# Graph attention: features and turned probabilities in fp32, one fp32 product per block in place of three fp16 products

## The reference, cut to what matters

```
h   = relu(layernorm(x))
Wh  = h @ W                                # the features
src, dst = Wh @ a[:F], Wh @ a[F:]          # two scores a node
att = softmax(where(adj > 0, leaky_relu(src + dst.T), -9e15), axis=1)
h_prime = att @ Wh                         # the product that is changed
gi, gh = h_prime @ w_ih.T + b_ih, h @ w_hh.T + b_hh
r, z, n = ...                              # gates and candidate of the GRU
x = x + (1 - z) * n + z * h
```

## Time and profile before

| | |
|---|---|
| median of 3 runs | 3374.41 us (3373.42 to 3374.91) |
| time of the profiled execution | 3378.01 us |
| its span, first to last instruction | 3376.3 us |
| `attention_features`, first product to last score column | about 51 to 95 us in the span |
| `gat_gru`, first adjacency tile to last update | about 120 to 609 us |
| PE, DVE, ACT busy over the whole span | 74%, 63%, 38% |

### The profile page before, as it was taken

The page is one execution under the profiler, slowest core; times in us unless marked ns, Lnnn a source line. Parts: engine busy times, 40 slices in busy tenths (PEclk is TensorE's granted clock), DMA queues, the critical chain, the costliest instruction groups (busy, mean ns, idle before and its releaser), DMA issues. The chain is left out here.

```text
span 3376.3 us, 47607 instructions
## 1 busy us (share of the span) xinstructions
PE 2512.2 (74%) x14938; PEld 1795.0 (53%) x14938; DVE 2112.2 (63%) x5159; ACT 1270.4 (38%) x2109; POOL 588.6 (17%) x1525
## 2 busy tenths in 40 slices
PE   3488888395749997968754596397748159999999
PEld 2366667384527775757623375275537024444458
DVE  5578887413246667673237777777785767777751
ACT  4455554303256564632245375275532320000000
POOL 0000000000033333320025364264430000000000
PEclk9699999697759998989856797697879579999999
DMA  1222220021000000000100000000000130000013
GB/s 41 105 87 90 92 96 30 25 63 47 15 1 16 20 23 14 17 20 16 39 15 5 5 14 14 5 14 9 9 9 10 37 101 0 0 0 0 0 33 96
DMA packets 44330, 104.10 MB, mean 31 GB/s; under 512 B 5584, under 2 KB 24304, under 8 KB 41328
## 3 DMA queue, kind: packets, MB, share of 16 engines
q1 hardware_dynamic: 44144, 102.05, 9.3%
HBM read 85.46 MB, written 16.58 MB: 30 GB/s over the span
## 5 line engine op out<-in xcount | busy, mean ns | idle before, releaser
L1206 PE MATMUL bank<-kT,step_queries 64*128 64x512 f32 x528 | 285.4, 693 | 315.1 <-ACT step_E L1273 299.8
L1705 DVE SCALAR_TENSOR_TENSOR fil_acc<-bank,fil_node,fil_acc 128x256 f32<-128x256 f32 x682 | 329.9, 484 | 109.9 <-PE bank L1778 97.3
L1206 PEld LDWEIGHTS bank<-kT,step_queries 64*128 64x128 f32 x528 | 107.5, 228 | 491.0 <-ACT step_E L1273 413.2
L1273 ACT ACTIVATE step_E<-bank 128x512 f32<-128x512 f32 (+1 forms) x264 | 137.4, 545 | 412.6 <-PE bank L1206 209.8
L1776 PE MATMUL bank<-fil_wh,fil_xTh 128*128 128x512 f16 x704 | 268.1, 381 | 0.0
L1777 PE MATMUL bank<-fil_wl,fil_xTh 128*128 128x512 f16 x704 | 267.9, 380 | 0.0
L1778 PE MATMUL bank<-fil_wh,fil_xTl 128*128 128x512 f16 x704 | 267.8, 380 | 0.0
L1293 ACT ACTIVATE step_junk<-step_E,step_first 128x2708 fp8e4<-128x2708 f32 x88 | 224.6, 2552 | 14.7 <-ACT step_bell L1300 8.9
L1386 DVE MAX8 step_top<-step_E 128x8 f32<-128x2708 f32 x44 | 131.2, 2982 | 132.9 <-ACT step_E L1273 128.4
L1223 PE MATMUL bank<-H,step_PT 128*128 128x256 f32 x968 | 212.6, 379 | 0.8 <-ACT step_PT L1264 0.8
L1223 PE MATMUL bank<-A,step_PT 128*128 128x256 f32 x968 | 212.6, 379 | 0.7 <-ACT step_PT L1264 0.7
(11 more groups left out here) (339 smaller groups left out, 5433.6 us busy)
## 6 DMA issues: line engine op xcount, KB each, us to landing
gat_A<-in_adj SPq DMA_DIRECT2D x22, 1408.0 KB, 6.1
step_a<-adjT SPq DMA_DIRECT2D x44, 352.0 KB, 3.1
fil_raw<-in_L_W SPq DMA_DIRECT2D x16, 512.0 KB, 4.8
adjT<-gat_a SPq DMA_DIRECT2D x22, 352.0 KB, 2.2
gcn_a<-adjT SPq DMA_DIRECT2D x22, 352.0 KB, 3.0
out_a<-adjT SPq DMA_DIRECT2D x22, 352.0 KB, 2.9
X<-in_x SPq DMA_DIRECT2D x1, 2816.0 KB, 10.9
x_kept<-X SPq DMA_DIRECT2D x1, 2816.0 KB, 9.8
```

The lines of the kernel that those rows point to most:

```text
L1206: pe.matmul(l_bank[n % 2][:, 0:m], queries[q][half, :], kT[half, c:c + m], start=True, stop=True).then_inc(l_ready, 1)
L1273: act.activation(E[q][j][:, c:c + m], l_bank[n % 2][:, 0:m], ACT.Copy).then_inc(l_done, 1)
L1705: c(dve.scalar_tensor_tensor(out=acc[k][:], in0=ps, scalar=node[k][:, n:n + 1], in1=acc[k][:], op0=ALU.mult, op1=ALU.add))
```

## The change

The features are kept as fp32 rows `V` (ACT copies the bank, no low half on DVE). The turned probabilities are copied by ACT as fp32 into `PT`, which takes the same memory as the four fp16 halves did; DVE's six low halves a tile go. The product of a block is one fp32 matmul call. The waits on `lo_done` become waits on `pT_done`, which ACT's copy raises. The scale factors of the fp16 parts go. `probabilities_times`, which nothing called, is deleted.

```diff
-            def high(t, k):
+            def rows(t, k):
                 act.wait_ge(wh_ready, t + 1)
-                core.fence(act)
-                act.activation(hi(HLw, t), wh_bank[k][:, 0:D], ACT.Copy, scale=SH).then_inc(hi_done, 1)
+                act.activation(cols(V, t), wh_bank[k][:, 0:D], ACT.Copy).then_inc(rows_done, 1)
...
                 reuse(dve, scored, t, 2)
-                dve.wait_ge(hi_done, t + 1)
-                dve.scalar_tensor_tensor(out=lo(HLw, t), in0=ps, scalar=SH, in1=hi(HLw, t),
-                                         op0=ALU.mult, op1=ALU.subtract)
+                dve.wait_ge(rows_done, t + 1)
...
-        PhT = [core.HL[:, k * NP:(k + 1) * NP] for k in range(2)]
-        PlT = [core.HL[:, (2 + k) * NP:(3 + k) * NP] for k in range(2)]
+        PT = [core.HL[:].bitcast(F32)[:, k * NP:(k + 1) * NP] for k in range(2)]
...
-            lows = [(1, lambda t, k, n=n: low(t, k, n)) for n in range(NCH)]
-            pipelined(dve, [(3, take_product), (0, mask), *lows[0:2], (1, row_scale), (6, update), (4, gates),
-                            (5, candidate), lows[2], (0, larger), *lows[3:5], (0, probabilities), lows[5]])
+            pipelined(dve, [(3, take_product), (0, mask), (1, row_scale), (6, update), (4, gates),
+                            (5, candidate), (0, larger), (0, probabilities)])
...
-                act.activation(PhT[k][:, b * 128:(b + m) * 128], p_bank[n % 2][:, 0:m * 128],
-                               ACT.Copy, scale=SP).then_inc(hi_done, 1)
+                act.activation(PT[k][:, b * 128:(b + m) * 128], p_bank[n % 2][:, 0:m * 128],
+                               ACT.Copy).then_inc(pT_done, 1)
...
-                    pe.wait_ge(lo_done, t * NCH + n - 1)
+                    pe.wait_ge(pT_done, t * NCH + n - 1)
...
                 if n == 0:
-                    pe.wait_ge(lo_done, t * NCH + NCH)
+                    pe.wait_ge(pT_done, t * NCH + NCH)
...
-                    pe.matmul(ps, PhT[k][:, blk], hi(HLw, j), start=j == 0, stop=False)
-                    pe.matmul(ps, PhT[k][:, blk], lo(HLw, j), start=False, stop=False)
-                    last = pe.matmul(ps, PlT[k][:, blk], hi(HLw, j), start=False, stop=j == T - 1)
+                    last = pe.matmul(ps, PT[k][:, blk], V[:, j * D:j * D + D], start=j == 0, stop=j == T - 1)
```

More of the change, by code:

```diff
@@ L39 @@
 SH = 1024.0
-SP = 8192.0
 SX = 8.0
@@ L316, in times_weight, with attention_features @@
     return last
-def attention_features(core, HLw, S, dB, dpB, dmin, W, a):
+def attention_features(core, V, S, dB, dpB, dmin, W, a):
     nc, HL, idh = core.nc, core.HL, core.idh
@@ L325, in attention_features @@
         sem = lambda n: nc.alloc_semaphore(f"wh_{n}")
-        loaded, xt_ready, xT_ready, wh_ready, hi_done, scores, scored, rep_ready, dB_done, tail, stored = (
-            sem(n) for n in ("loaded", "xt_ready", "xT_ready", "wh_ready", "hi_done", "scores", "scored",
+        loaded, xt_ready, xT_ready, wh_ready, rows_done, scores, scored, rep_ready, dB_done, tail, stored = (
+            sem(n) for n in ("loaded", "xt_ready", "xT_ready", "wh_ready", "rows_done", "scores", "scored",
                              "rep_ready", "dB_done", "tail", "dB_ready"))
@@ L371, in evacuate @@
                 act.activation(xT[k][:], xt_bank[k][:, 0:D], ACT.Copy, scale=1 / SH).then_inc(xT_ready, 1)
-            def high(t, k):
+            def rows(t, k):
                 act.wait_ge(wh_ready, t + 1)
-                core.fence(act)
-                act.activation(hi(HLw, t), wh_bank[k][:, 0:D], ACT.Copy, scale=SH).then_inc(hi_done, 1)
-            pipelined(act, [(0, evacuate), (1, high)])
+                act.activation(cols(V, t), wh_bank[k][:, 0:D], ACT.Copy).then_inc(rows_done, 1)
+            pipelined(act, [(0, evacuate), (1, rows)])
             for n, (b, m) in enumerate(CHUNKS):
@@ L410, in _ @@
             dve.tensor_scalar(dpB[:], dB[:], dmin[:, 0:1], None, ALU.subtract)
[L413 to L421, removed]
 def adjacency_times(pe, ps, a8, V, start=True):
@@ L431, in adjacency_times, with gat_gru @@
     return last
-def gat_gru(core, HLw, S, dpB, dmin, adj, adjT8, w_ih, w_hh, b_ih, b_hh):
+def gat_gru(core, V, S, dpB, dmin, adj, adjT8, w_ih, w_hh, b_ih, b_hh):
     nc, X, H = core.nc, core.X, core.H
@@ L446, in gat_gru @@
             sem(n) for n in ("masked", "small", "exp_done", "merged", "p_ready", "rs_ready"))
-        pT_ready, hi_done, lo_done = sem("pT_ready"), sem("hi_done"), sem("lo_done")
+        pT_ready, pT_done = sem("pT_ready"), sem("pT_done")
         aT_ready, a8_done, deg_ready, hc_ready = (sem(n) for n in ("aT_ready", "a8_done", "deg_ready", "hc_ready"))
@@ L538, in probabilities @@
                                          op0=ALU.mult, op1=ALU.mult, accum_out=sk(k, 7)).then_inc(p_ready, 1)
[L540 to L545, removed]
             def take_product(t, k):
@@ L551, in take_product @@
                 dve.wait_ge(pv_ready, t + 1)
-                dve.tensor_scalar(hp[k][:], pv_bank[k][:, 0:D], rs[:, k:k + 1], 1 / (SP * SH),
-                                  ALU.mult, ALU.mult).then_inc(hp_ready, 1)
+                dve.tensor_scalar(hp[k][:], pv_bank[k][:, 0:D], rs[:, k:k + 1], None,
+                                  ALU.mult).then_inc(hp_ready, 1)
                 dve.tensor_copy(core.deg[:, bass.ds(t, 1)], pv_bank[k][:, D:D + 1]).then_inc(hp_ready, 1)
@@ L602, in steep, with turned @@
                 act.activation(P[k][:, 0:N], P[k][:, 0:N], ACT.Exp, bias=sk(k, 5)).then_inc(exp_done, 1)
-            def high(t, k, n):
+            def turned(t, k, n):
                 b, m = CHUNKS[n]
@@ L633, in tanh @@
                 act.activation(inn[k][:], inn[k][:], ACT.Tanh).then_inc(n_done, 1)
-            turned = [[(1, lambda t, k, n=n: high(t, k, n)), (0, lambda t, k, n=n: adjacency(t, k, n))]
+            copies = [[(1, lambda t, k, n=n: turned(t, k, n)), (0, lambda t, k, n=n: adjacency(t, k, n))]
                       for n in range(NCH)]
-            pipelined(act, [*turned[0], *turned[1], (0, gentle), *turned[2], (0, steep), (3, features), *turned[3],
-                            (4, sigmoids), *turned[4], (5, tanh), *turned[5]])
+            pipelined(act, [*copies[0], *copies[1], (0, gentle), *copies[2], (0, steep), (3, features), *copies[3],
+                            (4, sigmoids), *copies[4], (5, tanh), *copies[5]])
         @block.tensor
@@ L1843, in build @@
         with ExitStack() as ctx:
-            HLw = core.sb("HLw", [128, T * 2 * D], F16, ctx)
+            V = core.sb("V", [128, T * D], F32, ctx)
             S, dmin, dpB = (core.sb(n, [128, m], F32, ctx) for n, m in (("S", T), ("dmin", 1), ("dpB", NP)))
@@ L1847, in build @@
             with ExitStack() as c:
-                attention_features(core, HLw, S, core.sb("dB", [128, NP], F32, c), dpB, dmin, L0_W, L0_a)
-            gat_gru(core, HLw, S, dpB, dmin, adj, adjT8, L0_w_ih, L0_w_hh, L0_b_ih, L0_b_hh)
+                attention_features(core, V, S, core.sb("dB", [128, NP], F32, c), dpB, dmin, L0_W, L0_a)
+            gat_gru(core, V, S, dpB, dmin, adj, adjT8, L0_w_ih, L0_w_hh, L0_b_ih, L0_b_hh)
         degrees(core)
```

## The result

The median is now 3338.61 us (3334.55 to 3347.38, 5 runs) against 3374.91 us (3373.42 to 3383.48, 5 runs) for the kernel before: ratio 0.989, 95% interval 0.987 to 0.991. The forecast was 3374.7, range 3369.5 to 3381.5. The profiled execution took 3347.38 us (span 3345.6), the slowest of its five; before it was 3378.01.

The account below looks back on a forecast made before the run. PE's ordered list, with two waits inside it, was taken to bound the attention. Attention -6.8 + 11.05 + 3.8 = +8.05 us and features -7.8 gave +0.25 us on a 3374.41 median: about 3374.7, range 3369.5 to 3381.5.

Parts of the forecast that it names:

- only two stretches can move: Whole kernel: only the features (51 to 95 us) and the attention with its GRU (120 to 609 us) can change.
- The features give nothing: Rival, features: no gain there, as PE or ACT is as late as DVE; 3382.5 us, chance 0.05.
- DVE sets the pace: Rival, attention: the 3.8 us a tile taken off DVE come through, PE's extra is hidden; 3357 us, chance 0.04.
- the chain: Steady attention tile: PE's ordered list from chunk 4 of the adjacency to the next exponential sets the pace; +0.65 us a tile.
- The period: Steady attention: exponentials every 21.05 us instead of 20.40, +11.05 us over 17 tiles.
- the transition from 16 bits to fp32: PE, product shares behind bf16 turns (rounds 1 and 3 to 5): the first fp32 instruction costs 0.09 us extra a round.
- one pass less: Rival, attention product: an fp32 block costs half, 0.216 us, so PE's path shrinks; 3322 us, chance 0.02.
- The first tiles: Attention start, to the exponential of step 4: product starts earlier, idle stretch and low clock shrink; -6.8 us.
- The last steps: Attention end: 48 blocks dearer by 0.104 us and five transitions, less two waits; +3.8 us.
- The features: Features stage, bound by DVE: line 392 and its register work go, 0.34 to 0.44 us for two tiles; -7.8 us.
- my bound of 8.8: Features: upper end of the saving, 0.44 us each over the 20 times in which DVE is the bound.
- no change: Whole kernel: time the same within 0.2% (6.7 us), chance 0.79.

Follow-up runs that it names:

- after_nobranch: The changed kernel with the repair and tie-pass branch of both diffusion steps never entered: 3090.02 us, ratio 0.9145 to the kernel before.
- after_dve_work: The changed kernel with six operations a tile, shaped like the low halves, put back on DVE on an unawaited buffer: 3350.82 us, one execution.

## Why the prediction was wrong

The step that failed is the first: "The rest of the kernel is not touched, so only two stretches can move." The code was not touched; its input was. The last bits of the first layer's output decide how often the branch runs. Passes in the trace and time, DVE's lists as they were or as the change has them: 9 gives 3375 to 3377, 8 gives 3360 (the doubled tolerance, one execution), 7 gives 3338.6, 6 gives 3314 and 3320. The changed product loses two passes: 19.0 and 18.1 us in the profiled pair, about the 36 us between the medians. I could have seen it in the profile of before: nine tie passes in two stages of 22 like tiles each, and in the first of them one interval of 44.98 us among those of 26.02. None of my rivals had it. "The features give nothing", "DVE sets the pace" and the others were all about the changed stretch.

Inside the layer the chain held, with terms of another size. The sizes that were off follow, one by one.

*The period*: 21.05 predicted, 20.97 measured ((540.25 - 183.75) / 17), so 9.7 us and not 11.05. Exponentials of the kernel after (timeline, ACT), the first ones and the last:

```profile
129.02 2.55 ACT L574 ACTIVATE gat_E<-gat_P,gat_sm 128x2708 f32<-128x2708 f32 x1 [0.62 <-DVE gat_sm L511]
145.87 2.55 ACT L574 ACTIVATE gat_E<-gat_P,gat_sm 128x2708 f32<-128x2708 f32 x1
162.78 2.55 ACT L574 ACTIVATE gat_E<-gat_P,gat_sm 128x2708 f32<-128x2708 f32 x1 [0.63 <-DVE gat_sm L511]
183.75 2.55 ACT L574 ACTIVATE gat_E<-gat_P,gat_sm 128x2708 f32<-128x2708 f32 x1
...
540.25 2.56 ACT L574 ACTIVATE gat_E<-gat_P,gat_sm 128x2708 f32<-128x2708 f32 x1
```

The mis-sized term is the transition from 16 bits to fp32. PE in the kernel after, one tile:

```profile
296.08 0.40 PE L641 MATMUL bank<-idb,gat_A 128*128 128x128 bf16 x4 [1.20 <-ACT gat_a L595]
296.32 1.95 PE L662 MATMUL bank<-V,HL 128*128 128x256 f32 x8
298.10 0.38 PE L628 MATMUL bank<-idf,gat_P 128*128 128x128 f32 x2
...
304.23 1.46 PE L662 MATMUL bank<-V,HL 128*128 128x256 f32 x6
305.52 0.60 PE L628 MATMUL bank<-idf,gat_P 128*128 128x128 f32 x4
...
306.19 1.95 PE L662 MATMUL bank<-V,HL 128*128 128x256 f32 x8
307.97 0.60 PE L628 MATMUL bank<-idf,gat_P 128*128 128x128 f32 x4
```

Share 0 stands behind the fp32 gates: 6 instructions in 1.29 us, 0.215 each. Shares behind bf16 turns take 1.78 us for 8: 8 x 0.216 + 0.05. I had taken 0.09 from one product of the features, behind fp16 turns. The kind of turn alone doesn't explain the difference: in the kernel after the features' third product, also right behind fp16 turns, takes 55.79 - 54.87 = 0.92 us, which is 0.06 above the stream. Two transitions at 0.05 instead of 0.09 take the 0.65 to 0.57, the measured difference of the periods. A block is 0.432 us, and the one wait left is for the adjacency copy, 1.20 us (1.3 predicted, though 1.75 less the 1.3 of the prediction's own working would leave 0.45: before, a second wait of 0.53 us for the same copies stood at 307.28, 2.28 in all). None is for the copy of the probabilities. The rival "one pass less" falls with it. A block is four times the 0.109 us of one fp16 product, as in the Trainium skill's page FP8 and Floating Point Precision (TensorE Precision Notes). The Trainium skill's page Perfetto Trace Analysis (Engine Utilization, footnote to the table) gives half the output rate for what it calls FP32_LOW_HIGH; one instruction here, 0.216 us, is at half the fp16 rate, and a block is two of them. No row names that mode.

*The first tiles*: -6.8 predicted, -7.0 measured. Between the second exponential and the fifth it was 61.70 us before (140.06 to 201.76) and is 54.73 (129.02 to 183.75): -6.97. The steps in between agree too: 157.4 and 174.1 less the 11.04 us by which everything is earlier give 146.4 and 163.1; measured 145.87 and 162.78. The product runs through the stretch in which the clock fell before. Windows, columns as in rows 1:

```profile
140.00:142.00 2.00, 2.00 (x9) 1.40 (x8) 1.81 (x4) 0.00 (x0) 0.00 (x0) 0.50 0.07 23
142.00:144.00 2.00, 2.00 (x12) 1.84 (x11) 2.00 (x1) 1.19 (x2) 0.00 (x0) 0.87 0.93 287
146.00:160.00 14.00, 12.58 (x98) 10.49 (x97) 7.91 (x7) 9.63 (x12) 0.00 (x0) 1.00 0.14 41
160.00:180.00 20.00, 18.23 (x120) 14.33 (x119) 13.46 (x23) 10.25 (x13) 0.40 (x1) 1.00 0.39 152
```

*The last steps*: +3.8 predicted, +3.2 measured (61.39 us from the last exponential to the degrees before, 64.55 after). Five smaller transitions are 0.2 of the missing 0.6; the rest stays open.

*The features*: -7.8 predicted, -11.0 in this pair (140.06 to 129.02). DVE, its scores of three pairs of tiles (timeline, DVE):

```profile
57.78 0.42 DVE L391 SCALAR_TENSOR_TENSOR wh_scr<-bank,wh_a 128x256 f32<-128x256 f32 x1 [0.20 <-ACT V L374]
60.56 0.42 DVE L391 SCALAR_TENSOR_TENSOR wh_scr<-bank,wh_a 128x256 f32<-128x256 f32 x1
63.30 0.42 DVE L391 SCALAR_TENSOR_TENSOR wh_scr<-bank,wh_a 128x256 f32<-128x256 f32 x1
```

2.74 us for two tiles, then, and not the 2.9 to 3.05 that I gave; before 3.74, and 3.70 in the later pairs. That is close to 1.0 us a pair. The rest is TensorE's rate at the start of the stage. The same product of the second tile, before and after:

```profile
53.65 2.02 PE L314 MATMUL bank<-wh_W,wh_xT 128*128 128x256 f32 x4
```
```profile
53.67 1.14 PE L313 MATMUL bank<-wh_W,wh_xT 128*128 128x256 f32 x4
```

The first product takes 2.07 us in both; the second is still slow before, and not after. The record of the granted clock gives 1.00 for both from 44 to 56 us, so it doesn't show this; the durations do. In the two kernels without the branch the second product takes 1.14 and 1.15 us, and there the last score column comes 9.8 us earlier (92.75 to 82.94), more than my bound of 8.8 for the 0.34 and the 0.099 us together. The first tile's gentle exponential comes 8.7 us earlier (121.99 to 113.31); where the 1.1 us between go is open.

So the layer is worth 5.1 us in the profiled pair, with that help, where the forecast was +0.25: features 3.2 better, period 1.3, the ends 0.8. Without the branch it is worth 2.0 us, as the second product of the features is then as fast before as after. With the branch out nothing measurable is left of it (3088.52 against 3090.02, the spreads overlap). Of this pair "no change" was right, in part by luck, since the stage behind the layer took back what the layer gave; of the kernel it was wrong.

## The clock behind an idle stretch

What I had not expected: how late the full clock can come. In the stage behind the layer PE idles from 780 to about 817 us, where the granted clock falls to 0.50 (1.2 GHz), then works with hardly a gap. The kernel after:

```profile
818.00:820.00 2.00, 1.95 (x11) 1.36 (x9) 0.00 (x0) 0.77 (x2) 0.00 (x0) 0.50 1.04 347
820.00:840.00 20.00, 20.00 (x92) 16.56 (x91) 2.00 (x8) 3.66 (x14) 0.00 (x0) 0.53 0.29 96
840.00:842.00 2.00, 1.69 (x15) 1.42 (x13) 0.13 (x1) 0.38 (x1) 0.00 (x0) 1.00 0.00 0
```

The kernel with its blocks reversed, the same instructions at the same time:

```profile
818.00:820.00 2.00, 1.95 (x12) 1.45 (x12) 0.00 (x0) 0.77 (x2) 0.00 (x0) 0.50 1.03 348
820.00:840.00 20.00, 18.87 (x137) 15.48 (x136) 3.20 (x12) 5.68 (x21) 0.00 (x0) 0.94 0.30 100
840.00:842.00 2.00, 2.00 (x18) 1.66 (x16) 0.17 (x1) 0.43 (x2) 0.00 (x0) 1.00 0.00 0
```

92 matmuls in 20 us against 137. The clock came up at about 839 in the one and 822 in the other, though both began near 818. From the layer's end to the first logits the first takes 311.5 us, the second 304.1. Of the twelve profiled kernels three have the long form (after, after_nobranch, after_dve_work: 311.1 to 312.4 us), nine the short one (302.7 to 305.4). All three are fp32 kernels, but the reversed one is too, and is short. The end of the layer doesn't sort them: 604.8 and 608.9 are long, 605.3 and 607.7 short. What decides stays open, since each kernel has one profiled execution. In the profiled pair without the branch it takes back 6.7 us (311.1 against 304.4), more than the 2 us of the layer; that it does so in the other executions is not shown. It is large enough to make up half of the spread from 3334.55 to 3347.38 among runs of one kernel, which is not shown either.

## What to carry to other kernels

Before saying "the rest is untouched", look for branches on data behind the edit: equal tiles with unequal intervals, or a line whose count doesn't fit its loop. If there is one, an edit that alters rounding can alter the time, and then neither sign nor size says anything of the edit's own work. Measure with the branch out, or over several roundings of the same work, before crediting an instruction. And price a lighter engine at the tiles where the pipeline fills, apart from the steady ones: the DVE work was worth some 4 us in two tiles and nothing in seventeen.
